# A two-layer decoder on one core: another hand-fixed order of the same steps on all engines

## The reference

```python
x = _layernorm(x + _L0_attn_ref(...))    # chunked memory attention (chunks of 64 tokens)
x = _layernorm(x + _L0_xattn_ref(...))   # causal self attention, cross attention to ctx, small ffn
x = _layernorm(x + _L0_ffn_ref(...))     # router, 8 experts (4 of them per token), one shared expert
x = _layernorm(x + _L1_attn_ref(...))    # delta rule in chunks of 32, four FIR paths, router
x = _layernorm(x + _L1_xattn_ref(...))   # cross attention to ctx
x = _layernorm(x + _L1_ffn_ref(...))     # 4 different dense experts, weighted by a router
```

```python
A = jnp.einsum('bhncd,bhned->bhnce', kbc, kc)
T = eye + jnp.tril(A, -1)                                  # 32 x 32, per batch row, head and chunk
inv = jax.scipy.linalg.solve_triangular(T, eye, lower=True, unit_diagonal=True)
u, w = inv @ vc, inv @ kbc
# then over the 4 chunks: att, u_adj = u - w @ S, o = q @ S + att @ u_adj, S = S + k^T u_adj
hmid = gelu(concat([x, fir3, fir7, fir15, fir31, delta_out]) @ router_W1 + b1)    # 768 -> 256
probs = softmax(hmid @ router_W2 + b2)                     # weights of the five paths
```

## Time and profile before

| | us |
|---|---|
| median of 3 runs | 1003.74 |
| lowest and highest | 1002.26, 1004.86 |
| span of the profiled execution | 1004.1 |

### The profile page before, as it was taken

One profiled execution on the slowest core, in us unless ns is written; L12 is line 12 of the kernel. 1 busy time (PEld: TensorE's weight loads), 2 busy tenths in 40 slices (PEclk: granted clock), 3 DMA queues, 4 the chain that ended last, 5 costly groups with the idle time before them and its releaser, 6 DMA issues.

```text
span 1004.1 us, 22014 instructions
## 1 busy us (share of the span) xinstructions
PE 932.3 (93%) x7958; PEld 593.9 (59%) x7958; DVE 742.6 (74%) x2882; ACT 650.3 (65%) x1474; POOL 334.5 (33%) x720
## 2 busy tenths in 40 slices
PE   6988899999986989999999999999977899999996
PEld 3877574644433556677876656665334555677674
DVE  3556789899899986866374797869999996665514
ACT  5699899866442236679898867765432356787653
POOL 4765342625022012736243331141340022342232
PEclk7999999999987799999999999999986999999998
DMA  9400002030453120100000000223443200000001
GB/s 308 175 2 1 1 1 52 2 83 14 95 128 75 43 70 17 44 22 12 1 12 1 11 11 1 53 60 94 90 97 76 57 21 22 2 11 1 12 1 32
DMA packets 77692, 45.44 MB, mean 45 GB/s; under 512 B 53008, under 2 KB 68880, under 8 KB 77328
## 3 DMA queue, kind: packets, MB, share of 16 engines
q1 hardware_dynamic: 77584, 44.04, 16.5%
HBM read 33.01 MB, written 11.01 MB: 44 GB/s over the span
## 4 chain that ended last, share of the span: by engine, by line
PE 57%; DVE 27%; ACT 8%; POOL 4%; issue 3%; DMA 0%; SPq 0%; POOLq 0%; ACTq 0%; DVEq 0%
PE psum L1101 7%; DVE pool L1588 5%; DVE sol_t L1593 5%; PE psum L558 5%; PE psum L1091 4%; PE psum L859 4%; PE psum L833 3%; PE psum L831 3%; PE psum L994 3%; DVE pool L1531 3%; PE psum L920 3%; PE psum L1085 2%; PE psum L1087 2%; ACT pool L1823 2%; PE psum L567 2%
## 5 line engine op out<-in xcount | busy, mean ns | idle before, releaser
L1809 ACT ACTIVATE pool<-psum 128x512 f32<-128x512 f32 x144 | 84.0, 595 | 64.4 <-PE psum L558 22.4
L2185 POOL TENSOR_SCALAR small<-small 128x4 f32<-128x4 f32 x88 | 22.2, 252 | 283.6 <-DVE small L1173 281.4
L1823 ACT ACTIVATE pool<-pool,small 128x128 f32<-128x128 f32 x224 | 91.5, 486 | 27.3 <-POOL small L2190 27.1
L558 PE MATMUL psum<-sb_const,pool 128*128 128x128 f32 x672 | 100.9, 283 | 6.4 <-ACT pool L1823 2.9
L920 PE MATMUL psum<-pool,firw 128*32 128x512 f32 (+7 forms) x960 | 103.2, 571 | 0.0
L558 PEld LDWEIGHTS psum<-sb_const,pool 128*128 128x128 f32 x672 | 79.3, 145 | 37.9 <-issue 22.3
L2188 POOL TENSOR_TENSOR small<-small,minus_half 128x4 f32<-128x4 f32 x88 | 92.2, 1048 | 7.3
L994 PE MATMUL psum<-pool,sb_l1a 128*128 128x512 f32 x192 | 88.6, 612 | 0.0
L1101 PEld LDWEIGHTS psum<-sb_l1f,pool 128*128 128x128 f32 x640 | 77.2, 192 | 11.3 <-issue 9.5
L1101 PE MATMUL psum<-sb_l1f,pool 128*128 128x128 f32 x640 | 82.8, 278 | 0.0
L1404 DVE TENSOR_TENSOR pool<-pool,psum 128x512 f32<-128x512 f32 x80 | 52.4, 682 | 37.8 <-ACT pool L2095 16.2
(11 more groups left out here) (429 smaller groups left out, 2139.5 us busy)
## 6 DMA issues: line engine op xcount, KB each, us to landing
pool<-scratch_kk SPq DMA_DIRECT2D x18, 256.0 KB, 3.8
pool<-in_cF SPq DMA_DIRECT2D x16, 256.0 KB, 3.1
scratch_kk<-pool SPq DMA_DIRECT2D x10, 256.0 KB, 2.6
pool<-in_xF SPq DMA_DIRECT2D x8, 256.0 KB, 6.2
pool<-in_x SPq DMA_DIRECT2D x8, 256.0 KB, 7.0
scratch_xt<-pool SPq DMA_DIRECT2D x8, 256.0 KB, 2.0
pool<-scratch_xt SPq DMA_DIRECT2D x8, 256.0 KB, 3.2
scratch_kk<-pool SPq DMA_DIRECT2D x32, 64.0 KB, 1.9
```

Source lines behind the costliest of these rows:

```text
L558: m = e.transpose(f.ap[:, part(b)], src[:, part(b)], ident)
L1809: e.activation(slot(g, i), f.ap, ACT.Copy).then_inc(f.emptied, 1)
L1823: m = e.activation(dst[:, part(b)], src[:, part(b)], ACT.Identity, bias=v["nm"][:, b:b + 1], scale=v["r"][:, b:b + 1])
```

## The change

Only the string `ORDER` is replaced: 86 lines become 99, so every line below it has a number higher by 13 in the changed kernel (line 1593 is 1606, 1588 is 1601, 994 is 1007). Every step of every group is still listed exactly once, and each engine gets the same instructions in another order, but for the table loads on ACT, which follow from it: 89 before, 96 after. The bank of each product also follows from the table. Of the diff two lines of before and one of the change stand for the rest:

```diff
@@ -36,99 +36,112 @@
...
-b_x.54/5 b_fir.2/7 b_x.1-2/6 b_x.55/5 b_x.3-4/6 b_x.56/5 b_x.5-6/6 b_x.57/5 b_x.7-8/6 b_x.58/5 b_x.9/6 b_x.59/5
-b_x.10/6 b_x.60-61/5 b_x.11-14/6 b_xo/5 b_x.15/6 b_u.2/4 b_x.16-17/6 b_rs/5 b_x.18-31/6 b_fir.3/7 b_xt/5 b_p.2/4
...
+b_x.38-44/5 b_x.0/6 b_x.45/5 b_x.1/6 b_x.46/5 b_fir.1/7 b_x.2/6 b_x.47/5 b_x.3/6 b_x.48/5 b_x.4/6 b_x.49/5 b_x.5/6
...
```

196 lines of the change are left out of this document (105 added, 91 removed).

## The result

The changed kernel takes 1015.41 us (median of 4 runs, 1013.91 to 1016.47), the kernel before 1004.22: a ratio of 1.0108, 95% interval 1.009 to 1.0126. Forecast were 992 and a range of 983 to 1004. Run again on another occasion (e12) it took 1013.03 beside 1006.32, ratio 1.0068 (1.0043 to 1.0092). So it is slower by 0.4 to 1.3%, and the forecast was wrong in its sign.

A forecast was written before the change was run, and what follows sets the result against it. DVE was taken to bound the two solve waves and TensorE the full stretches; -6.3 - 4.6 - 5.4 + 2.6 + 1.5 = -12.2 us from 1004.1 gave 991.9, rounded to 992, range 983 to 1004.

The forecast's parts named there:

- What bounds the kernel: DVE, never waiting, paces the two solve stretches (waves, 263-355 and 734.5-793.3 us); TensorE work alone counts in the full stretches.
- term A: Alternating groups' solve instructions on DVE saves 115 ns per broken-up same-group pair: -6.3 us wave one, -4.6 us wave two.
- Rival 1: Alternating solves gives nothing because DVE's pipe empties after every instruction: 1002.8 us, chance 0.07.
- Term B: Exit of wave one: 11.8 us of TensorE work pulled ahead, 6.4 us of DVE work along with it, net -5.4 us.
- Term C: ACT's table loads rise from 89 to 96; two fall into group 0's router chain in the mixed stretch: +2.6 us.
- Term D: Blocks' turn through DRAM before each solve, about 8 us, barely covered by 8.9 to 10.2 us of DVE work: +1.5 us.
- The rest: 0: Reordered first 184 us, where TensorE idles 11.9 us, counted at 0, bounds -6 and +6; unchanged last steps 0.
- The clock: 0: No gain or loss: DVE-paced waves do not quicken with a higher clock, and outside them it is already 1.00.
- The slower rival: Full stretch, 376.6 to 697.2 us, leaks as late activations hold up TensorE: +25.3 us, giving 1017; chance 0.13.
- Rival 2: Covers too thin: DRAM turn +6 and table loads +9.0, or wave one's exit gain halved: some 997.5 us, chance 0.15.

The follow-up runs named there:

- e12: The changed kernel once more, unchanged, against the kernel before: 1013.03 us beside 1006.32, ratio 1.0068.
- e15: Kernel before with the changed order of wave two only, but all groups' solve steps in the sequence of before: 1010.03 us, ratio 1.0046.
- e16: Kernel before with the changed exit of wave one and 14 early TensorE products, but all solve steps in the sequence of before: 1004.08 us, ratio 1.0.
- e2: Kernel before with only the changed order from b_vs/0, before the first solve, to b_lg/2, after wave one: 1004.61 us, ratio 0.9999.
- e8: Kernel before with only the changed order from b_x.44/1 to b_lg/2, the exit of wave one: 1002.5 us, ratio 0.9983.
- e1: Kernel before with only the changed opening, its first 109 steps: 1011.86 us, ratio 1.0056.
- e7: Changed kernel with 118 more TensorE products, results overwritten, at eight places in wave two: 1015.79 us, ratio 1.0117.
- e3: Kernel before with only the changed order between the waves, from b_lg/2 to b_x.44/4: 1012.1 us, ratio 1.0074.
- e4: Kernel before with only the changed order of wave two, from b_x.44/4 to y_pT/4: 1009.59 us, ratio 1.0045.

## Why the prediction was wrong, point by point

- **What bounds the kernel: right as a reading of before, wrong as a law.** DVE did not wait in the waves, so DVE work was priced at its full duration. PE was at 80% in wave two at a clock of 0.80, and its products feed every DVE step there: they were ready 2.2 us ahead at b_kk/7 and 1.2 at b_p.2/5, less than the 4.6 us to be taken out. The step "all of it on DVE, all in stretches where DVE never waits" failed, and with it the price of term A. I should have asked for each DVE step of the wave how long its products had been ready in before, and put the smaller of that and the gain into the sum.
- **Term A, -10.9 us.** The price per pair held to the nanosecond (34 and 82 for 34 and 81), the count too. On DVE 3.4 us were found from b_x.0/5 to b_oT/5 and 3.6 from b_x.0/1 to b_oT/1; in the time, nothing in wave two (e15) and 0.6 of 3.3, give or take 1.8, in wave one (e16). Rival 1 (alternating gives nothing) had the outcome right for its part and the reason wrong.
- **Term B, -5.4 us.** Wave one with its exit, solves included, did win in the traces, 4 to 8 us from 200 to 300 us of work, but alone it was worth 0 (e2) or 1.7 us (e8, not clear of zero). TensorE's idle time from 263 to 355 us fell by 3.9 us, from 18.0 to 14.1, where the prediction wanted 8 or more. Of the 11.8 us pulled ahead, the bound "0, if the chain of group 3 holds the pulled products back" was the nearer one. In the changed kernel DVE waits 5.7 us between b_oT/1 and b_oT/2, where before it was 3.0.
- **Term C, +2.6 us.** 96 loads as counted. PE's waits for ACT between 30 and 180 us grew by about 1.6 us (the largest groups 5.3 before, 6.9 after), within the 3 named. Not tested alone.
- **Term D, +1.5 us.** Right: the two waits at copies that start a solve are 1.0 us (group 3) and 0.4 (group 7), 1.4 in all, the others none.
- **"The rest: 0".** With wave two the largest error. The first 45 us were reordered too, and I set them to 0 with bounds of 6 either way for the whole mixed stretch; the opening alone is +7.2 in the trace and +5.6 (2.9 to 8.3 by the ratio's interval) as e1. The bounds came from TensorE's idle time in a window that begins at 27 us, so they left out the place where the loss arose. And idle time was the wrong measure: it is alike in both openings (2.7 and 2.9 us between 12 and 22), the clock is not.
- **"The clock: 0".** This step failed in the opening: "outside the waves it is at 1.00 already" overlooks the first slice, which has a 7 in the clock row, and there the changed order has 12.1 us more at the lower clock, an estimated 6 us. It was also argued that a wave paced by DVE gains nothing by a higher clock. In wave two the time at the lower clock went from 24 to 41 us, and over seven traces DVE's waits grow with it, from 5.4 to 8.8. e7 (clock 1.00 for 0.81, same time) does not speak against that, since its filling took some 26 us itself.
- **The slower rival.** 1017 was named, at a chance of 0.13, and 1015.4 came. But its mechanism, a leak in the full stretch, is not what the changed kernel's trace shows: 318.84 of 320.6 us there, 0.5% idle where the prediction named 1.5% as its sign, and some 2.8 us lost by work. e3's 1012.1 by itself would speak for it; by its trace most of that lies at the cut. What came instead was the loss in the opening and in wave two. (Rival 2's sum comes to 997.4, not 997.5.)

How the parts stand to the whole: opening +5.6, wave one 0, middle +7.4 of which 6.9 by the table belong to the cut, wave two +4.5, by the ratios of e1 to e4 times 1004 us: 10.6 to 17.5 against 6.8 to 10.8 measured for the change whole. They don't add up exactly. The changed kernel wins 8.3 in wave one after having come late to it, e2 alone wins 4 to 6 there, so a late arrival may be partly made good.

In the prediction's terms: wave two was forecast at -4.6 and cost +4.5, wave one with its exit at -11.7 and gave 0 to -1.7, the opening at 0 and cost +5.6.

Open are: what in the new opening keeps the clock low for longer; whether in wave two the waiting follows the clock or the clock the waiting, and which moved step starts it; and the share of the table loads.
